# Wider spacing of hand-overs in the first pass, gate logits by moving nodes, and an earlier start of the main pass's first table, one-hots and gathers

## The reference

```python
x = x + gnn(layernorm(x))          # xn @ W1.T + b1 + mean(xn[dst] over the edges of src) @ W2.T + b2
x = x + ffn(layernorm(x))          # for each node n:
#   shared  = relu(relu(n @ sW1 + sb1) @ sW2 + sb2) @ sW3 + sb3      256 -> 256 -> 128 -> 256
#   expert e (4 of them): the same form                              256 -> 128 -> 64 -> 256
#   gates = softmax(n @ gW + gb)   # 4 logits; the two best experts, reweighted by a softmax
#   ffn   = shared + sum over the two best of weight * expert
```

## Time and profile before

| what | value |
|---|---|
| median of 3 runs | 3321.48 us (3320.13 to 3323.53) |
| the profiled execution | 3327.94 us, span 3326.4 us |
| busy, share of the span | PE 95%, PEld 87%, DVE 81%, ACT 58%, POOL 55% |
| mean granted TensorE clock | 0.979 of full |
| chain that ended last | PE 70%, POOL 1%, all else 0% |
| matmuls of the logits, line 1135 | 1600, first half 135.9 us busy, second 144.1 us |
| indirect DMAs of `scatter`, line 308 | 400, 541.4 us busy, mean 1354 ns |
| `rstd`, line 296 | 50, 90.3 us busy, mean 1806 ns |
| `count_chunk`, two each of lines 383, 390, 397 | mean 406, 1239, 399 ns |
| `stats`, eight each of lines 341, 348; `low`, two of line 370 | mean 408, 148; 671 ns |
| `edges_low`, line 1263; `x1T_hi`, line 1201 | mean 1487; 577 ns |

### The profile page before, as it was taken

How to read it: one execution, slowest core, us unless ns; L and a number is a source line. 1 busy time by engine, 2 the same in 40 slices (tenths; PEclk the granted TensorE clock), 3 DMA queues, 4 the chain that set the end, 5 groups by cost and what they waited for, 6 DMA issues and landing times.

```text
span 3326.4 us, 62783 instructions
## 1 busy us (share of the span) xinstructions
PE 3149.4 (95%) x21617; PEld 2897.3 (87%) x21617; DVE 2689.4 (81%) x7213; ACT 1920.7 (58%) x3407; POOL 1819.3 (55%) x1554
## 2 busy tenths in 40 slices
PE   6989889888949999999999999999999999999998
PEld 6989889888949898988989898898989889898987
DVE  7888888885338888888888888888888888888885
ACT  4555555555625656566565656556565655656564
POOL 0688888888155454555545455555455555554540
PEclk9999999999969999999999999999999999999999
DMA  7676666666543332323333232333333233332320
GB/s 230 187 199 185 180 187 190 192 195 171 160 116 89 91 96 83 96 83 99 90 93 94 83 95 83 98 87 94 96 82 97 82 99 87 95 94 86 94 76 26
DMA packets 201860, 387.47 MB, mean 116 GB/s; under 512 B 106703, under 2 KB 109853, under 8 KB 201538
## 3 DMA queue, kind: packets, MB, share of 16 engines
q1 hardware_dynamic: 133938, 226.03, 24.4%
q10 hardware_dynamic: 30800, 102.42, 9.5%
q0 software_dynamic: 36800, 54.95, 7.0%
HBM read 236.11 MB, written 161.00 MB: 119 GB/s over the span
## 4 chain that ended last, share of the span: by engine, by line
PE 70%; POOL 1%; issue 0%; DVE 0%; ACT 0%; DMA 0%; POOLq 0%; DVEq 0%
PE acc L1071 25%; PE acc L1122 13%; PE acc L1041 12%; PE acc L1135 5%; PE acc L1054 4%; PE acc L1052 4%; PE acc L1095 3%; PE acc L1118 1%; PE acc L1087 1%; PE acc L1081 1%; POOL rows L1423 0%; POOL e_oh L1435 0%; ACT h2f L1170 0%; ACT h_hi L1180 0%; DVE rows L1507 0%
## 5 line engine op out<-in xcount | busy, mean ns | idle before, releaser
L1423 POOL DMA_INDIRECT rows<-z_d,tab x500 | 562.8, 1126 | 633.8 <-DMA tab<-tab_d 461.5
L1435 POOL TENSOR_SCALAR e_oh<-iota_sb,tab 128x250 fp32r<-128x250 f32 (+1 forms) x500 | 521.4, 1053 | 534.3 <-PE acc L1054 534.1
L1071 PE MATMUL acc<-x1T_hi,wl_hl 128*128 128x500 f32 x2400 | 666.9, 392 | 0.0
L308 POOL DMA_INDIRECT tab_d<-pair,idx x400 | 541.4, 1354 | 118.9 <-issue 108.7
L632 PE MATMUL acc<-w_hl,xT_hi 128*125 128x256 f32 x3200 | 585.9, 289 | 0.3
L1071 PEld LDWEIGHTS acc<-x1T_hi,wl_hl 128*128 128x128 f32 x2400 | 444.4, 189 | 85.6
L632 PEld LDWEIGHTS acc<-w_hl,xT_hi 128*125 128x125 f32 x3200 | 481.5, 194 | 0.6 <-issue 0.6
L1122 PE MATMUL acc<-wl_hl,h_hi 128*125 128x256 f32 x2400 | 480.6, 282 | 0.0
L1321 DVE TENSOR_TENSOR h_lo<-h1f,h_hi 128x500 fp32r<-128x500 f32 x600 | 397.4, 675 | 74.8 <-ACT h_hi L1164 47.9
L1157 ACT ACTIVATE h1f<-acc,bl_sb 128x500 f32<-128x500 f32 x600 | 405.8, 676 | 48.4 <-PE acc L1071 42.8
L1122 PEld LDWEIGHTS acc<-wl_hl,h_hi 128*125 128x125 f32 x2400 | 394.9, 187 | 0.0
(11 more groups left out here) (143 smaller groups left out, 6591.7 us busy)
## 6 DMA issues: line engine op xcount, KB each, us to landing
xs<-in_x SPq DMA_DIRECT2D x100, 448.0 KB
z_d<-zs ACTq DMA_DIRECT2D x100, 448.0 KB
y_d<-ys ACTq DMA_DIRECT2D x100, 448.0 KB
y_sb<-y_d SPq DMA_DIRECT2D x100, 448.0 KB
x_sb<-in_x SPq DMA_DIRECT2D x100, 448.0 KB
out<-x_sb SPq DMA_DIRECT2D x100, 448.0 KB
codes_b<-code_d SPq DMA_DIRECT2D x25, 390.6 KB
rows<-z_d,tab POOLq DMA_INDIRECT x500
```

What stands on the lines that cost most here:

```text
L308: pool.indirect_dma_start(out=tab_d, out_offset=bass.IndirectOffsetOnAxis(ap=idx[:, n:n + 1], axis=0), in_=pair[:, 2 * n:2 * n + ROW], in_ ...
L1071: mm = pe.matmul(bank[L1_BANKS[t]][:, 0:GN], wl1_hl[:, w, f, t * P:(t + 1) * P], (x1T_hi, x1T_lo)[a][:, f, :], start=n == 0, stop=n == 5)
L1423: pool.indirect_dma_start(out=rows[g.h][:, q, :], out_offset=None, in_=z_d, in_offset=bass.IndirectOffsetOnAxis(ap=tab[g.h][:, q, 0:1], ax ...
L1435: pool.tensor_scalar(e_oh[:, q, w], iota_sb[:, w], tab[g.h][:, q, 1:2].bitcast(F32), None, ALU.is_equal).then_inc(S["e_oh_ready"], 1)
```

## The change

- First pass. DVE's order becomes `low(g+1)`; `neg_bias((g+3)/2)` for odd g (one group earlier); `stats(g/2+2)` for even g, ahead of `slots` and `count_chunk`; `slots` two groups later. PE gathers counts two groups back instead of one, from 4 buffers instead of 3 (`OB`). ACT does `norm(g+2)` ahead of the first `half_rows`. x is loaded 6 groups ahead, not 4. `G_SCAT` is 8, and two of a group's five scatters stand ahead of `rstd`. The edge arithmetic at the start uses the memory of `rows`, and one copy of `c_h` goes.
- Logits. `gw_hl` is widened to 128 columns (zeros beyond 8) and becomes the stationary operand; the 500 nodes move, in four matmuls to bank 1 behind `sum_edges`. ACT copies the result to `lgT_sb`, and behind layer 3 four transposes bring it to bank 5, where DVE reads it with a stride of 128.
- Start of the main pass. `tab`, `rows`, `e_oh` and their semaphores are made at the top. At the end of the first pass SP loads tables 0 and 1 once all scatters landed; POOL makes the one-hots of group 0, waits for the stores of z, and gathers group 0. DVE clears `rows` in groups 89 and 90.

```diff
-G_SCAT = 6
+G_SCAT = 8
+OB = 4
-        gw_hl = sb("gw_hl", [P, 2, FT, 8], F32R)
+        gw_hl = sb("gw_hl", [P, 2, FT, P], F32R)
...
# SP, first pass
-                            if 6 <= g + 4 < NG and g + 4 >= XB:
-                                load_x(g + 4)
+                            if g + XB < NG:
+                                load_x(g + XB)
...
+                        sp.wait_ge(s_alltab, 1)
+                        load_table(sp, G(0, 0))
+                        load_table(sp, G(0, 1))
                         for h in range(ZB):
                             sp.wait_ge(s_y[h], LOAD * len(range(h, NG, ZB)))
                             sp.wait_ge(s_z[h], LOAD * len(range(h, NG, ZB)))
# POOL, first pass
                         for g in range(NG):
+                            if g >= G_SCAT:
+                                n = (g - G_SCAT) * PER_G
+                                for e in range(n, min(n + 2, EC)):
+                                    scatter(e)
                             if g % 2 == 0 and g + 4 < NG:
                                 rstd(g // 2 + 2)
                             if g >= G_SCAT:
-                                n = (g - G_SCAT) * PER_G
-                                for e in range(n, min(n + PER_G, EC)):
+                                for e in range(n + 2, min(n + PER_G, EC)):
                                     scatter(e)
                         for h in range(NSC):
                             pool.wait_ge(s_scat[h], 16 * (EC // NSC))
+                        pool.nop().then_inc(s_alltab, 1)
+                        pool.wait_ge(s_cst, 16 * 5)
+                        edges_onehots(pool, G(0, 0))
+                        for h in range(ZB):
+                            pool.wait_ge(s_z[h], LOAD * len(range(h, NG, ZB)))
+                        pool.wait_ge(S["cleared"], 2)
+                        gather(pool, G(0, 0))
# DVE, first pass (count_chunk: own16[:, k % OB], waits for s_sel >= k - OB + 1 from k = OB)
                             if g + 1 < NG:
                                 low(g + 1)
-                            if g % 2 == 0 and g + 2 < NG:
-                                neg_bias(g // 2 + 1)
-                            if (done + 1) * BATCH - 1 <= last_chunk(g - 1) and done < NCH // BATCH:
+                            if g % 2 and g + 3 < NG:
+                                neg_bias((g + 3) // 2)
+                            if g % 2 == 0 and g + 4 < NG:
+                                stats(g // 2 + 2)
+                            if (done + 1) * BATCH - 1 <= last_chunk(g - 3) and done < NCH // BATCH:
                                 slots(done)
                                 done += 1
                             for k in chunks_of(g):
                                 count_chunk(k)
-                            if g % 2 == 0 and g + 4 < NG:
-                                stats(g // 2 + 2)
                             if G_WTS <= g < G_WTS + 5:
                                 low_weights(g - G_WTS)
+                            elif G_WTS + 5 <= g < G_WTS + 7:
+                                dve.wait_ge(s_flat, 3)
+                                dve.memset(rows[g - G_WTS - 5][:], 0.0).then_inc(S["cleared"], 1)
# ACT, first pass
                                 high(g + 1)
+                            if g + 2 < NG:
+                                norm(g + 2)
                             half_rows(g, 0, zs, 4, s_z, a_z)
                             half_rows(g, 0, ys, 2, s_y, a_y)
-                            if g + 2 < NG:
-                                norm(g + 2)
# PE, first pass
-                            if g:
-                                for k in chunks_of(g - 1):
+                            if g >= 2:
+                                for k in chunks_of(g - 2):
                                     gather_counts(k)
...
# PE, main pass, between sum_edges(3) and layer 3
+                if nxt:
+                    if back:
+                        pe.wait_ge(S["h2_relu_ready"], i.n(H2T, 2))
+                    n = 0
+                    for part, t in enumerate((x1T_hi, x1T_lo)):
+                        for f in range(FT):
+                            mm = pe.matmul(bank[1][:, 0:GN], gw_hl[:, part, f, :], t[:, f, :],
+                                           start=n == 0, stop=n == 3)
+                            n += 1
+                    mm.then_inc(S["lgT_done"], 1)
# PE, main pass, behind layer 3
+                    pe.wait_ge(S["lgT_ready"], n1.n(1, 1))
                     for s in range(NS):
-                        n = 0
-                        for part, t in enumerate((x1T_hi, x1T_lo)):
-                            for f in range(FT):
-                                mm = pe.matmul(bank[5][0:SP_, s * 8:(s + 1) * 8], ...)
-                                n += 1
+                        mm = pe.transpose(bank[5][0:SP_, s * P:(s + 1) * P],
+                                          lgT_sb[:, s * SP_:(s + 1) * SP_], ident_sb[:])
                     mm.then_inc(S["lgN_done"], 1)
# ACT, main pass, between h2_high(2) and edges_high
+                if nxt:
+                    act.wait_ge(S["lgT_done"], n1.n(1, 1))
+                    if n1.c:
+                        act.wait_ge(S["lgN_done"], n1.n(1))
+                    act.copy(lgT_sb[:], bank[1][:, 0:GN]).then_inc(S["lgT_ready"], 1)
# POOL, main pass
-                if (i + 3).exists():
+                if (i + 3).exists() and i.c > -3:
                     edges_onehots(pool, i + 3)
...
-                    gather(pool, G(0, 0))
...
-                    for h in range(2):
-                        dve.memset(rows[h][:], 0.0).then_inc(S["cleared"], 1)
```

More of the change, by code:

```diff
@@ new lines, in build, with __init__, __add__, exists @@
+        S = {n: sem(n) for n in names}
+        class G:
+            def __init__(self, k, c):
+                self.k, self.c = k, c
+                self.h, self.u = c % 2, c % U
+            def __add__(self, d):
+                return G(self.k, self.c + d)
+            def exists(self):
+                return not isinstance(self.k, int) or 0 <= self.c < NG
+            def at(self):
+                return self.k * U + self.c
+            def of(self, t):
+                return t[self.at()] if isinstance(self.k, int) else t[bass.ds(self.at(), 1)][0]
+            def n(self, per, done=0):
+                return self.k * (U * per) + (self.c * per + done)
+            def half(self, per):
+                return self.k * (U // 2 * per) + (self.c // 2 + 1) * per
+            def quarter(self, per):
+                return self.k * per + (self.c // U + 1) * per
@@ new lines, in load_table, with gather @@
+        def load_table(sp, g):
+            if g.c >= 2:
+                wait_alone(sp, S["e_oh_ready"], (g + -2).n(EQ, EQ))
+                wait_alone(sp, s_rows[g.h], (g + -2).half(16 * EQ))
+            sp.dma_start(tab[g.h][:], g.of(tab_v)).then_inc(s_tab[g.h], 16)
+        def gather(pool, g):
+            wait_alone(pool, s_tab[g.h], g.half(16))
+            if g.c >= 2:
+                wait_alone(pool, S["e_lo_ready"], g.n(1, -1))
+            for q in range(EQ):
+                pool.indirect_dma_start(
+                    out=rows[g.h][:, q, :], out_offset=None, in_=z_d,
+                    in_offset=bass.IndirectOffsetOnAxis(
+                        ap=tab[g.h][:, q, 0:1], axis=0),
+                    bounds_check=N - 1, oob_is_err=False).then_inc(s_rows[g.h], 16)
@@ L108, in build, with edges_onehots @@
+        def edges_onehots(pool, g):
+            if g.c:
+                wait_alone(pool, S["agg_done"], g.n(NS))
+            wait_alone(pool, s_tab[g.h], g.half(16))
+            for q in range(EQ):
+                w = slice(WINDOW[q][0] * SP_, WINDOW[q][1] * SP_)
+                pool.tensor_scalar(e_oh[:, q, w], iota_sb[:, w],
+                                   tab[g.h][:, q, 1:2].bitcast(F32), None,
+                                   ALU.is_equal).then_inc(S["e_oh_ready"], 1)
         with ExitStack() as c1:
@@ L186, in build @@
                 s_flat = sem("flat_arrays_ready")
+                s_half = sem("halves_ready")
                 s_tr = sem("edge_arrays_transposed")
@@ L502, in _ @@
                         stats(1)
+                        neg_bias(1)
                         low(0)
@@ L723, in _ @@
                         with sp.If(mode > 1):
+                            for h in range(2):
+                                sp.wait_ge(s_tab[h], 16)
                             for k in range(NFILL):
@@ L943, in build @@
         with ExitStack() as c2:
-            tab = [sb(f"tab{h}", [P, EQ, ROW], I32, c2) for h in range(2)]
-            rows = [sb(f"rows{h}", [P, EQ, D], F32, c2) for h in range(2)]
             y_sb = [sb(f"y_sb{h}", [SP_, NS, D], F32, c2) for h in range(2)]
```

145 lines of the change are left out of this document (54 added, 91 removed).

## The result

The changed kernel takes 3266.97 us (median of 4 runs, 3266.21 to 3267.21), the kernel before 3321.17 beside it: a ratio of 0.9837 (95% interval 0.9824 to 0.9849), 54 us faster. 3266 was predicted. The profiled execution took 3267.08 us with a span of 3265.5; the one of before was 3327.94, 6.8 above its median, so the two traces differ by more than the medians do.

What follows compares the result with a forecast made beforehand. PE was taken to bound the main pass and POOL 734 us of the first; hand-overs -6, start -14 and logits -36 make -56 us, from a median of 3321.5 to 3266, with 3238 to 3292 for 8 in 10.

Steps and rivals of the forecast that it cites:

- The bound of the main pass: Main pass: PE is busy 100%, so each 0.01 us taken from its step is 1 us of the kernel.
- The logits: Main pass, PE: 1.29 us of new work replaces 1.66; 0.36 a step over 100 steps, -36 us.
- Start of the main pass: Between the passes: early tables, one-hots and gather of group 0 start PE 13.8 us earlier; -14 us.
- can be loaded at once: Second step of the main pass: table 2 can now be loaded at once; before, a POOL gather waited for it.
- So the lead is kept: Second step of the main pass: PE's earlier start is not lost again, giving -14 us.
- again late by the same amount: Second step of the main pass: POOL, with gathers 1 and 2 and then one-hots, is as late against PE as before.
- Hand-overs: First pass: -14.5 us behind the last scatter, +14.5 in front, -4 and -2 from earlier work; sum -6 us.
- -20 to +15: First pass: ends given for the stage since scatter length under DVE's new order was unknown; 0 taken for that effect.
- Rival (B): First pass: scatters get shorter, half their excess over the median goes, -32 us, 3234; chance 0.09.
- Rival (A): First pass: DVE and POOL wait in a ring, 2.5 us idle in 40 rounds, +100 us, 3366; chance 0.05.
- Rival (D): Main pass: the clock falls with 16 transposes a step; a tenth of steps slow is +220 us, 3486; chance 0.02.

Runs made afterwards that it cites:

- e1: The kernel before with the logits part alone, both passes' orders as before: 3279.05 us, ratio 0.9874.
- e4: The changed kernel with SP loading table 2 ahead of the loads of y and x for groups 0 and 1: 3260.65 us, ratio 0.9818.
- e3: The changed kernel with logits and hand-overs put back, leaving only the early tables, one-hots and gather of group 0: 3317.7 us, ratio 0.9986.
- e2: The kernel before with the hand-overs of the first pass alone: 3313.75 us, ratio 0.9983.
- e8: e4 with POOL's one-hots of group 1 and power of group 0 ahead of the gather of group 2: 3257.65 us, ratio 0.9808.
- e5: The changed kernel with the same 400 scatters spread over 90 groups instead of 80: 3211.66 us, ratio 0.9665.
- e9: The changed kernel with e5, e4 and e8 together: 3199.06 us, ratio 0.9634.
- e6: The changed kernel without every second set of eight scatters, 200 instead of 400: 3148.36 us (2 runs), ratio 0.9479.

## Why the prediction came out right, point by point

**The bound of the main pass: right.** PE is busy throughout, no other engine makes it wait from 1000 to 3150 us, and a gain per step came out once per step.

**The logits: right in mechanism, a little small.** Predicted were 1.29 us for the new work and 0.36 a step. Measured: 1.25 and 0.40. From one layer 1 to the next over the whole pass the traces differ by 42.8 us. 97 steps give 38.8; the first gives 1.2 and the second last 2.9, and behind the last layer 1 come 1.7 more. The second last step has no `sum_edges`, and layer 3 waits for `h_lo`. Before and after:

```profile
3287.55 0.36 PE L1118 MATMUL acc<-b_r,wT_r 128*125 128x256 f32 x1 [2.21 <-DVE h_lo L1333]
```

```profile
3231.09 0.38 PE L1186 MATMUL acc<-b_r,wT_r 128*125 128x256 f32 x1 [0.24 <-DVE h_lo L1403]
```

The new matmuls stand in front of layer 3 and fill most of that wait. I had priced every step like the one in the middle and left out these ends. Alone, the part is worth 41.6 (e1) where 36 was forecast. The cover was judged well: the copy has 4.0 us where 3.7 was expected, the gate weights 1.4 where 1.2 was, and DVE's wait moved to line 1449, the former 1379, though into it and not in front of it. Of the about 131 ns for 512 moving columns in the Trainium skill (TensorE: Matmul & The Clock Gate, Back-to-back issue gap) nothing shows here: 0.89 us for four matmuls are 223 ns each, as in the earlier trace rows.

**Start of the main pass: the failed step.** It was sized at 14 and is worth 3 alone (2 to 8 by the interval). Down to the first `sum_edges` it held: the pause is 18.64 and ended by the low parts, 12.6 less (13.8 predicted). What failed is the sentence that table 2 "can be loaded at once", and with it "So the lead is kept". It can be *issued* at once, but in SP's order it stands behind the loads of y and x. Before, the table's buffer came free only with the one-hots of group 0; it was issued at 957.26 and landed in 2.1 us, when these loads were over (the last of them was issued at 939.35). The earlier one-hots freed the buffer at once, and so moved the table's issue into the burst of loads. I had named SP's loads of y and x and costed them only against their own reader, not against what stands behind them on the same queue. It landed in 9.8 us behind them and in 1.9 ahead of them, and e4 shows what that costs: 6.3 us. Of the rest of the 11, 1.2 were missing at the first `sum_edges` already, and 2.1 are POOL's: it isn't "again late by the same amount" in the second step even with the table early (e4). On rings the Trainium skill (DMA: Bandwidth & Descriptors, Queues, rings and completion order) says that each DMA engine consumes descriptors of a ring in order; the two landing times agree with it. No run separates the place in the queue from DMA engines that are simply busy with 2.0 MB and the gather of group 1, so that part of the cause stays open.

**Hand-overs: right sum, terms that erred both ways.** -6 was predicted, -7 measured alone. In front the scatters start 9.5 sooner (6 predicted). The wait after the first two scatters is 11.9 where 14.5 was put. Behind the scatters 20.4 are gone, not 14.5. The prediction counted 14 groups there before and 12 after; when the last scatter ends PE has in fact begun the transposes of all but 11 groups before and of all but 8 after, and in the end they follow at 7.03 us a group (895.55, 902.58) instead of 7.27. Against this the scatters grew by 0.033 us each, 13.6 us in this pair of traces. The size of this is uncertain: with the old hand-overs three traces (before, e1, e3) show means of 1.354, 1.372 and 1.368, with the new ones four (changed, e2, e4, e8) 1.387, 1.387, 1.386 and 1.389, which is 6 to 14 us for 400. But e5 and e9, with the new ones too and the scatters spread, show 1.373 and 1.364. So the longer scatters come with the new hand-overs where the scatters are packed, and which of the reordered engines makes them longer isn't shown. Scatters and powers together are 638.6 us against 631.7 before, 7 us more; that lies inside the -20 to +15 that I gave, though I took 0. Rival (B), shorter scatters, had its sign wrong. Rival (A) never took hold: from the power at 107.67 to the last scatter POOL doesn't wait for DVE. (The reading of the earlier trace rows left out two small rows of the same view, 9.9 us in 34 waits of 0.3 for the scatters' own DMAs and one more of 0.3 for DVE; each is as long as a gap for the issue, so nothing changes.) The wait is on the other side, DVE for POOL (`neg_bias`, 40 waits and 137.4 us from 80 to 870 us), which costs nothing while POOL is the bound.

**Rival (D)**: the granted clock stays at 1.00 in the main pass with 16 transposes a step. The first pass lost clock (0.96 to 0.92) without losing time: PE's busy time from 120 to 880 us rose only from 676 to 684 of 760 us, so idle time was left.

So that the total was hit to 1 us is partly luck: 11 us too much for the start and 6 too little for the logits cancel in part, and the rest lies within the spread. Not luck is the large term, the logits: its mechanism held. What the prediction saw and didn't use was larger than all of this: it said that 734 us of the pass hang on POOL and that 14 groups of PE's lie behind it (90 us in the trace). The conclusion, to spread the scatters to the end, is worth 55 us (e5), as much as the whole change.

## What to carry to other kernels

When work is moved to an earlier place, go through what it frees and starts, transfers and their place in the *issuing* queue too: a small load that gates the next stage goes ahead of the big ones. Where one engine carries a fixed amount of work that isn't tied to stages, it should reach from the first stage that can take it to the last: where it is packed into fewer stages it slows those, and the stages behind it run without using the engine. And price the first and the last rounds of a loop by their own rows.

## What the runs showed of the hardware

- A 40 KB table load lands in 1.9 to 2.1 us at the start of the main pass when nothing large is ahead of it in its queue, and in 9.8 us behind loads of 2.0 MB. From 1000 to 3150 us the median is 4.0 in the kernel before and 3.1 in the changed one.
- The length of an indirect scatter changes with what runs beside it: minimum 1.19 us in all kernels, mean 1.354 to 1.389 with all 400 of them, and 1.495 in e6, where the other engines take 18% less time a group beside 200 of them (15.35 us for two against 18.74). The Trainium skill (GPSIMD Engine Reference, Specifications) says that GpSimd shares its SBUF interfaces with VectorE, with contention against VectorE instructions in a 2-port mode or with two SBUF inputs. The mean of e6 goes that way (VectorE is busy 94% of its window, 76% of that of the changed kernel), but from before to the changed kernel the scatters grow while VectorE's share falls from 77% to 76%. No run here separates VectorE from the DMAs, so the cause stays open.
- Four transposes of a 128x125 tile take 0.36 us inside a stream, 0.09 each, less than the 0.104 of a matmul with 125 stationary and 8 moving columns.
- The power on POOL, with the same operands, takes 1.75 to 1.81 us on average with the old hand-overs (three traces) and 1.67 to 1.69 with the new ones (five), but 1.75 and 1.80 in e5 and e9, which have the new ones too. What sets it stays open.
